# Keys and queries of the first attention in 64x64 quarters, SyncE at the scatters' wait, half of the bias loaded in the expert stage

## The reference, cut to what matters

```
x = x + cross_attention0(layernorm(x), ctx)   # 8 heads; weights 64x64, they mix the 64 rows of a sequence
x = x + experts(layernorm(x))                 # each row: its 2 best of 8 experts, relu(x W_e + b_e), mean
x = x + cross_attention1(layernorm(x), ctx)   # 32 heads of 16, keys and values for 8
x = x + feed_forward(layernorm(x))            # silu(x Wg + bg) * (x Wu + bu), inner width 1376
```

## Time and profile before

| | |
|---|---|
| median of 3 runs | 890.0 us (886.49 to 892.05) |
| the profiled execution | 889.12 us, its span 887.4 us |
| TensorE busy | 846.3 us, 95% of the span |
| TensorE weight loads | 691.0 us, 78% |
| VectorE busy | 432.4 us, 49% |
| ScalarE busy | 347.0 us, 39% |
| GpSimd busy | 284.7 us, 32% |
| mean granted TensorE clock | 0.985 of full speed |
| stages | first attention 0 to 159 us, experts to 290, second attention to 505, feed-forward to the end |

### The profile page before, as it was taken

How to read it: one execution, slowest core, us unless ns; L and a number is a source line. 1 busy time by engine, 2 the same in 40 slices (tenths; PEclk the granted TensorE clock), 3 DMA queues, 4 the chain that set the end, 5 groups by cost and what they waited for, 6 DMA issues and landing times.

```text
span 887.4 us, 19751 instructions
## 1 busy us (share of the span) xinstructions
PE 846.3 (95%) x7585; PEld 691.0 (78%) x7585; DVE 432.4 (49%) x838; ACT 347.0 (39%) x567; POOL 284.7 (32%) x402
## 2 busy tenths in 40 slices
PE   5999997899999989999999899999999999999996
PEld 4888876688888867777777688878887888878885
DVE  4899973244444788888887621123211312122112
ACT  3666663233333456666666522321222122211110
POOL 3578885000000778777752221130020002002000
PEclk9999998799999999999999999999999999999999
DMA  8377679595553634544412431110030003011001
GB/s 284 131 252 254 229 251 288 171 322 199 166 164 113 197 122 135 170 143 144 118 50 58 137 119 38 45 33 1 18 114 12 1 13 107 0 49 47 1 0 48
DMA packets 55388, 105.28 MB, mean 119 GB/s; under 512 B 8226, under 2 KB 12322, under 8 KB 55042
## 3 DMA queue, kind: packets, MB, share of 16 engines
q1 hardware_dynamic: 48530, 85.02, 30.4%
q0 software_dynamic: 5120, 16.78, 5.7%
q10 hardware_dynamic: 1648, 2.23, 0.7%
HBM read 68.02 MB, written 35.98 MB: 117 GB/s over the span
## 4 chain that ended last, share of the span: by engine, by line
PE 73%; POOL 3%; issue 2%; DMA 2%; ACT 1%; DVE 1%; SPq 0%; DVEq 0%; ACTq 0%; POOLq 0%
PE c_ps L1273 9%; PE c_ps L1275 9%; PE c_ps L1274 9%; PE c_bank L1797 4%; PE c_bank L1311 3%; PE c_bank L1312 3%; PE c_bank L1317 3%; PE c_bank L1798 3%; PE c_bank L1803 3%; PE c_bank L1861 3%; PE c_bank L1010 2%; PE c_bank L1011 2%; PE c_bank L1016 2%; PE c_ps L1836 2%; PE c_po L1011 2%
## 5 line engine op out<-in xcount | busy, mean ns | idle before, releaser
L1350 DVE SCALAR_TENSOR_TENSOR d_hid<-c_ps,d_b_up,d_silu 128x512 f32<-128x512 f32 (+1 forms) x44 | 33.0, 751 | 227.9 <-PE c_ps L1275 227.9
L1273 PE MATMUL c_ps<-d_nT_hi,gate_up_hi 128*128 128x512 f32 (+1 forms) x352 | 139.9, 398 | 0.0
L1275 PE MATMUL c_ps<-d_nT_hi,gate_up_lo 128*128 128x512 f32 (+1 forms) x352 | 138.6, 394 | 0.0
L1274 PE MATMUL c_ps<-d_nT_lo,gate_up_hi 128*128 128x512 f32 (+1 forms) x352 | 138.3, 393 | 0.0
L1229 ACT ACTIVATE d_silu<-c_ps,d_b_gate 128x512 f32<-128x512 f32 (+1 forms) x44 | 30.3, 689 | 141.6 <-PE c_ps L1275 141.6
L1189 POOL TENSOR_TENSOR late_x<-late_x,d_b_down 128x512 f32<-128x512 f32 x16 | 20.9, 1340 | 188.8 <-DMA late_x<-x_after_attention 188.8
L1275 PEld LDWEIGHTS c_ps<-d_nT_hi,gate_up_lo 128*128 128x128 f32 (+1 forms) x352 | 65.2, 185 | 16.6
L1274 PEld LDWEIGHTS c_ps<-d_nT_lo,gate_up_hi 128*128 128x128 f32 (+1 forms) x352 | 65.4, 186 | 15.9
L1273 PEld LDWEIGHTS c_ps<-d_nT_hi,gate_up_hi 128*128 128x128 f32 (+1 forms) x352 | 65.3, 185 | 15.4
L1236 ACT ACTIVATE d_hid_hi<-d_hid 128x512 fp32r<-128x512 f32 (+1 forms) x44 | 27.8, 632 | 125.4 <-DVE d_hid L1350 125.4
L1040 ACT ACTIVATE b_rowsT_hi<-c_bank 128x512 fp32r<-128x512 f32 x39 | 23.4, 599 | 77.8 <-PE c_bank L999 77.8
(11 more groups left out here) (307 smaller groups left out, 1933.4 us busy)
## 6 DMA issues: line engine op xcount, KB each, us to landing
b_rows<-expert_rows SPq DMA_DIRECT2D x39, 256.0 KB, 2.7
expert_results<-b_result SPq DMA_DIRECT2D x39, 256.0 KB, 2.5
a_wstage<-L_ffn_W_e SPq DMA_DIRECT2D x16, 512.0 KB, 4.0
late_x<-x_after_attention SPq DMA_DIRECT2D x28, 256.0 KB, 4.0
c_stage<-gate_up SPq DMA_DIRECT2D x16, 344.0 KB, 3.4
out<-late_x SPq DMA_DIRECT2D x16, 256.0 KB, 2.8
x_after_attention<-late_x SPq DMA_DIRECT2D x12, 256.0 KB, 3.7
c_y_in<-x_after_attention SPq DMA_DIRECT2D x12, 256.0 KB, 2.8
```

What stands on the lines that cost most here:

```text
L1273: pe.matmul(bank[0:w, :], gu_hi[:, cols], nT_hi[:, g % 2, k, :], start=k == 0, stop=False)
L1274: pe.matmul(bank[0:w, :], gu_hi[:, cols], nT_lo[:, g % 2, k, :], start=False, stop=False)
L1275: mm = pe.matmul(bank[0:w, :], gu_lo[:, cols], nT_hi[:, g % 2, k, :], start=False, stop=k == KD - 1)
```

## The change

- `make_k` and `make_q` use `in_quarters`: sixteen products of 64x64, each with a quarter of the rows and the diagonal quarter of the weight that holds numbers. The results of both go into a pair of banks `pkq`, one bank for each sequence of the tile, the keys in the first 256 columns and the queries in the next. `wk` and `wq` aren't cleared any more, and ScalarE doesn't wait for `zeroed`.
- As the two share banks, `keep_k` waits for the queries, and `make_k` for the queries of the tile before to be kept. `transpose_x` writes into the scores' bank `ps` but for the last two tiles, and `make_scores` waits for the copy out of it.
- `load_o_consts` stands ahead of context 1 and x 2 in SyncE's list.
- The low part of the last expert weight goes from GpSimd to VectorE (`last_low_part`), and GpSimd scatters tile 12 at the end of round 16 instead of at its start. SyncE waits for all scatters instead of GpSimd.
- The first half of the bias is loaded in the expert stage, behind the rows of blocks 0 and 1.
- In the second attention `low_weights(3)` moves from the end of VectorE's round 0 into round 1; `invert_sums` and `keep_attn` of (14, 0) go ahead of the maximum of tile 15; TensorE's `project_low(13)` goes behind the attention of (14, 1), and VectorE's `add_attn(13)` behind its copy.

```
+        def xT_bank(t):
+            return ps if t + 2 < TILES else pk
...
-                sp.wait_ge(zeroed, 5)
+                sp.wait_ge(zeroed, 3)
...
             load_v_consts()
+            load_o_consts()
             load_ctx(1)
             load_x(2)
-            load_o_consts()
...
+                sp.wait_ge(scattered[i], 16 * TILES)
...
-            for buf in (wk, wv, wq, wo, wo_cross):
+            for buf in (wv, wo, wo_cross):
...
             for m in range(-2, TILES + 4):
-                if m >= TILES and tile(m - 4):
+                if m > TILES and tile(m - 4):
                     scatter(m - 4)
                 if tile(m + 2) or tile(m - 1):
                     scale_rows(m)
-                if tile(m - 1):
+                if tile(m - 1) and m < TILES:
...
-                if m < TILES and tile(m - 4):
+                if m <= TILES and tile(m - 4):
                     scatter(m - 4)
-            for i in range(2):
-                pool.wait_ge(scattered[i], 16 * TILES)
...
+            def in_quarters(which, rows, w):
+                for j in range(4):
+                    for b, r in ((0, 0), (1, 1), (0, 1), (1, 0)):
+                        k, head, at = slice(64 * b, 64 * b + 64), 2 * j + r, 256 * which + 64 * j
+                        mm = pe.matmul(pkq[64 * r:64 * r + 64, b, at:at + 64], rows[k, 64 * head:64 * head + 64], w[k, k], start=True, stop=True)
+                return mm
...
                 want(pe, k_kept, t)
-                want(pe, xt_kept, t - 3)
...
+                want(pe, q_kept, t)
+                in_quarters(0, ctx_in[t % 3], wk).then_inc(k_made, 1)
...
+                    pe.wait_ge(k_kept, 1)
                 pe.wait_ge(xn_ready, t + 1)
-                want(pe, q_kept, t)
...
+                in_quarters(1, xn[:, t % 2, :], wq).then_inc(q_made, 1)
...
+                want(pe, xt_kept, t - 2)
...
-                if tile(t + 3):
-                    pe.wait_ge(k_kept, t + 4)
+                if t + 2 < TILES:
+                    pe.wait_ge(s_shifted, t + 3)
                 else:
+                    pe.wait_ge(k_kept, TILES)
+                    pe.wait_ge(q_kept, TILES)
                     pe.wait_ge(xt_kept, t)
...
-                dve.wait_ge(k_made, t + 1)
+                    dve.wait_ge(k_made, 1)
+                else:
+                    dve.wait_ge(q_made, t + 1)
...
+            def last_low_part():
+                dve.wait_ge(w_hi, TILES)
+                dve.wait_ge(w_lo, TILES - 1)
+                high, low = expert_weights(TILES - 1)
+                dve.tensor_tensor(low, wstage[:, (TILES - 1) % 2, :], high.bitcast(F32), ALU.subtract).then_inc(w_lo, 1)
...
+                if m == TILES:
+                    last_low_part()
                 if tile(m - 1):
                     add_residual(m - 1)
...
+            if b == 1:
+                cols = slice(0, EXPERTS * DIM // 2)
+                sp.dma_start(bias[:, cols], b_e.rearrange("e h -> (e h)")[cols].partition_broadcast(P)).then_inc(shared["bias_loaded"][0], 16)
...
+                if m == TILES - 1:
+                    project_low(m - 2)
...
-                if 0 <= m - 1 < TILES:
+                if 0 <= m - 1 < TILES and m != TILES - 2:
                     project_low(m - 1)
...
+                if m == 1:
+                    low_weights(3)
...
+                if m < TILES:
+                    invert_sums(m, 0)
+                    keep_attn(m, 0)
                 if m == TILES - 2:
                     max_scores(m + 1, 0)
                     shift_scores(m + 1, 0)
-                if m < TILES:
-                    invert_sums(m, 0)
-                    keep_attn(m, 0)
```

More of the change, by code:

```diff
@@ L730, in by_position, with made @@
             def by_position(ap):
-                return ap.rearrange("p (j o) -> p j o", o=64)
-            every_bk, every_bq = (b[:, :].rearrange("p (x o) -> p x o", x=1).to_broadcast([P, 8, 64]) for b in (bk, bq))
+                return ap.rearrange("p (j b o) -> p b j o", b=2, o=64)
+            def made(which):
+                return pkq[:, :, 256 * which:256 * which + 256].rearrange("p b (j o) -> p b j o", o=64)
+            every_bk, every_bq = (b[:, :].rearrange("p (x y o) -> p x y o", x=1, y=1).to_broadcast([P, 2, 4, 64]) for b in (bk, bq))
             def keep_k(t):
@@ L746, in keep_q @@
                 want(dve, s_made, t)
-                dve.tensor_tensor(by_position(qT[:, :]), by_position(pq[:, :]), every_bq, ALU.add).then_inc(q_kept, 1)
+                dve.tensor_tensor(by_position(qT[:, :]), made(1), every_bq, ALU.add).then_inc(q_kept, 1)
             def all_scores():
@@ L2052, in _ @@
             for m in range(TILES + 2):
-                if 0 <= m - 2 < TILES:
+                if 0 <= m - 2 < TILES and m != TILES - 1:
                     add_attn(m - 2)
```

40 lines of the change are left out of this document (15 added, 25 removed).

## The result

The changed kernel takes 905.81 us (median of four runs, 904.62 to 908.86), the kernel before 889.42 beside it: a ratio of 1.018, 95% interval 1.014 to 1.021. It is slower by 16 us, where the forecast of 879.5 us was some 10 us less. The profiled execution has a span of 903.3 us against 887.4.

What follows compares the result with a forecast made beforehand. TensorE was taken to set the first attention's pace, VectorE 0.38 us a round behind; 889.12 - 4.9 - 4.2 - 0.9 = 879.1, with 0.9 for the median 880.0, rounded down to 879.5 us, range 876 to 882.5.

Steps and rivals of the forecast that it cites:

- step 1: First attention: quartered keys and queries cut rounds from 7.28 to 6.90 us, 4.9 us less over thirteen rounds.
- a drain: First attention: TensorE emptying at a change of tiling mode, estimated at 0.1 us each, leaving the sum the same.
- rival (a): First attention: the quarters bring nothing, rounds cost 0 instead of -4.9, 884.5 us; chance 0.11.
- Rival (d): First attention: slower, as TensorE's idle time lowers its granted clock to 1.2 GHz; four such rounds give 905; chance 0.04.
- The wait of `keep_k`: First attention: VectorE's new wait for the queries before copying keys is covered, with 0.3 us to spare.
- The start: Kernel start: fewer memsets and reordered loads change nothing, 0 us, between -1 and +2.5.
- The end of the stage: End of first attention: scatter 15 starts 1.1 us sooner and lands 3.1 us faster, together 4.2 us less.
- The landing: End of first attention: with the bias gone scatter 15 lands in 4.9 us instead of 8.0, 3.1 us less.
- Half of the bias in the expert stage: Expert stage: the 1 MB loaded there costs 0, up to +2 us.
- the rows of block 2: Expert stage: rows needed 8.6 us in, queued behind the bias's 1 MB; taken as 0, up to +2 us.
- Second attention: Last tiles of the second attention: scores come at 490.8 instead of 491.7, 0.9 us less; range -3 to 0.
- the stall of 2.11 us: Second attention, before 496.18: idle time of unshown cause that may stay or go, left out of the sum.

Runs made afterwards that it cites:

- e9_longer: The changed kernel, both passes quartered, with the product of the values done twice in each round; 888.72 us, 1.002 of the kernel before.
- e3_halves: The changed kernel with 8 products of 64x128 a pass in place of 16 of 64x64; 886.3 us, 0.999 of the kernel before.
- e6_full_waits: The changed kernel with four full 128x128 products a pass, new waits and transposes in the scores' bank kept; 882.76 us, 0.995 of the kernel before.
- e1_rest: The changed kernel without its quarters: full products for keys and queries, with the old waits and banks; 882.99 us, 0.996 of the kernel before.
- e4_spread: The changed kernel with the quartered queries moved behind the transposes of the probabilities; 896.57 us, 1.011 of the kernel before.
- e10_bias_in_stage: e1_rest with both halves of the bias loaded at the end of the first attention as before; 884.56 us, 0.996 of the kernel before.
- b1: q4 with the bias's first half back in the first attention, two key tiles sooner than in the kernel before; 880.13 us, 0.991 of the kernel before.
- k4: The changed kernel with only the keys in quarters, queries as four full products in the same banks; 882.88 us, 0.9955 of the kernel before.
- q4: The changed kernel with only the queries in quarters, keys as four full products in the same banks; 879.05 us, 0.992 of the kernel before.
- e7_fewer_loads: The changed kernel without the loads of the experts' weights for tiles 2 to 15; 879.41 us, 0.992 of the kernel before.

## Why the prediction was wrong

**Quarters (step 1): wrong in sign, the rounds.** The step that failed is the price of the quartered passes, "Two are 1.26, so TensorE's round would be 7.28 - 0.62 = 6.66", taken for each of thirteen rounds in a row: the sum has no term for TensorE standing with its operands ready. The forecast was -4.9 us, and the rounds took +18.0. The price of a pass by itself was right: two passes in 1.09 us in the clean rounds (forecast 1.26), TensorE's own round 6.58 us (7.44 in e9_longer, 88.42 to 95.86, less the 0.86 from its first product of the values to its second; forecast 6.66), VectorE's round 6.85 (6.90), the way into the small tiles 0.10 us (e3_halves), the size that the forecast had assumed for a drain. In its place the runs showed that TensorE stands, with no wait that the profile names, where a round asks for some 45 instructions a us beside the loads of this stage: the passes took up to 3.0 us in seven of the ten long rounds, and in the three others the time went behind them. The earlier trace rows showed a count at the end of each row, x32 for the scores and x8 for the full keys; adding them up for a round, 216 before and 312 after (weight loads too), and dividing by its length, 29.7 a us against 45, would have shown that the change asks for half as many again; the densest stretch in the rows was the second attention with 35.4 (x2661 and x2647 in 150 us). What TensorE stands for stays open. The forecast named this under rival (a), "four times as many products pass through TensorE", priced it at nothing gained, and set it against the 0.63 us of a single pass, a row that can't show it: a burst of 32 records says nothing of what a whole round of them can keep up. Of the 18 us only some 3 are the clock, by an estimate: the four rounds with a granted clock below 1.00 (0.89, 0.74, 0.83, 0.82) take 38.4 us together, and four stalled rounds at 1.00 (of which there are six, 8.79 us in the mean) 35.2.

Rival (d) gave 905 us for the right reason in its last link only: the clock did fall in four rounds, yet only after the first stalled round, which ran at 1.00, and it has 3 us of the 18. That the number agrees is chance.

**The wait of `keep_k`:** right. e6_full_waits has it at no cost, where the queries come later than with quarters.

**The start: 0, measured +1.2** in the changed kernel and -0.9 in e1_rest, where the cleared weights are back. Within the bounds given (-1 to +2.5). The other runs with the new order of loads lie between -0.7 and +1.8, but e4_spread, whose queries come late, has +3.2.

**The end of the stage: -4.2, measured -2.6** with the disturbed rounds and -4.5 in e1_rest (37.26 to 32.77 us from the scores of tile 15). The split was off. In e1_rest scatter 15 didn't start sooner (its issue ended 28.3 us after the scores of tile 15, before 28.0): scatter 12 had been moved back, and scatter 14 waited 4.64 us for an earlier one to land, a wait that the forecast had left out. The landing gave 4.9 us, 4.43 in place of 9.30. e10_bias_in_stage shows that 3.1 of them are the megabyte's.

**Half of the bias in the expert stage: 0, measured +1.0 to +4.4** (e1_rest 1.0, the changed kernel 2.25, e6_full_waits 4.4, all at the twelfth block, against 0.2 in e10_bias_in_stage and 0.0 in b1). The bound of +2 was for the rows of block 2; but rows of the blocks ahead of them are late too (the wait of 1.21 us at 181.60), and the first reader of the bias begins 0.6 to 4.1 us later. Here a transfer that binds at the end of one stage binds at the start of the next one.

**Second attention: -0.9, measured -4.05.** The scores came 0.73 us sooner (forecast 0.9), and the rest is the stall of 2.11 us and what hung on it, which the forecast had left as a bound. e1_rest has the same 4.01 us between the scores and 10.09 to the feed-forward, so it doesn't hang on the rounds. What the stall was isn't shown. The kept trace of the kernel before adds one thing: an instruction packet of q8 ran from 493.92 to 494.86, inside the 2.11 us that ended at 496.18, and 450 of TensorE's instructions had begun since the last one landed, the highest count in any of the traces. This stall may be one of a late supply; one case doesn't show it.

**What is shown and what is open.** Shown: the loss needs both passes in quarters (e1_rest, k4, q4), and neither the new waits (e6_full_waits) nor how close the small products stand (e9_longer) makes it. It is gone or nearly gone when the same instructions are spread over longer rounds (e4_spread, 39.4 a us; e9_longer, 41.4) and when 7 MB of loads go (e7_fewer_loads, 45.4). Not shown: what TensorE waits for. Its instructions' count is known from parts 1 and 3 of the page of the changed kernel:

```profile
PE 850.2 (94%) x8353; PEld 684.2 (76%) x8353; DVE 432.3 (48%) x839; ACT 346.4 (38%) x567; POOL 283.0 (31%) x399
...
q8 instruction: 69, 1.13, 0.5%
```

and the page of e1_rest:

```profile
PE 842.6 (96%) x7585; PEld 687.7 (78%) x7585; DVE 433.9 (49%) x839; ACT 347.1 (39%) x567; POOL 284.4 (32%) x401
...
q8 instruction: 63, 1.03, 0.5%
```

The changed kernel has 768 products and 768 weight loads more (8353 records against 7585 each) and 6 packets more, 256 instructions a packet. All 69 packets hold 17,664 instructions at that rate, and the trace has 17,674 of TensorE, its waits included. The Trainium skill, "Runtime: NRT & Kernel Launch", section Instruction fetch mechanics, says that an engine's instructions come in blocks of 16 KiB, 256 instructions, by a queue of its own, and that the fetch is hidden. The packets agree with the first. The gaps don't speak against the second, as most of them have no packet beside them.

Two rivals are untested. GpSimd's first scatter starts at 52.44, in the first of the long rounds, and no run leaves the scatters out; they can't do it alone, as the runs without gaps have them too. And every run on record has a span and a granted clock, so each was recorded as it ran: a cost of recording each instruction would look the same, and no run here could tell. Open too is why the changed kernel gets 36.9 a us and not the 41.4 of e9_longer, and why its first rounds go through at 45.

## What to carry to other kernels

Before splitting products into small tiles, count the instructions of the whole round (products and weight loads, two of each for 32-bit numbers) and divide by the round that you hope for; compare that with the densest stretch of the kernel that is known to run clean beside the same loads, here about 40 a us. If the hoped-for round asks for more, it wants a run before it is counted on. A duration read from a short burst is the price of that burst and not of a round full of them. Where both passes don't fit, one may: with the queries alone in quarters, behind the long products of the keys, the kernel takes 0.992 of the time before, where the rest of the change by itself gives 0.996.

Where an idle time has no releaser and the supply of instructions is suspected, look at the times of the instruction packets in the same trace before calling it the cause.

A transfer moved out of a crowded end of a stage is paid for at the crowded start of the next; look for a stretch where the DMA engines are idle, or count it as no gain.

## What the hardware showed that was not expected

More work made the kernel faster: 1.018 of the kernel before without and 1.002 with a product of 0.86 us added to each round. A pass in row halves of 64x128 took 16 records of 60 ns and so no less than the 8 of the full one, while quarters of 64x64 over all four took 16 to 20, over two of the four 31. And an idle time of a weight load put down to "issue" is no stall where TensorE's products run on beside it: the 0.33 us ahead of the keys and the 0.8 ahead of the attention in e4_spread and e9_longer cost 0.1 us or nothing.
